# Expert tiles: one register load for three stagings, another order in the first steps, fewer products of zeros

## The chip, the cores and the metric

One core of a Trainium2 chip runs the whole program. Time is device microseconds from launch to end, median of three runs. TensorE is called PE, VectorE DVE, ScalarE ACT, GpSimd POOL, and SyncE SP.

## The reference

`x` is 4096 tokens of 256 features. The block is a macaron: half a mixture of experts, an attention with 16 heads, half the same mixture again.

```
def _L0_ffn_ref(x, gate_w, gate_b, w1, b1, w2, b2, w3, b3):
    logits = einsum('bsd,de->bse', x, gate_w) + gate_b
    probs = softmax(logits, axis=1)                 # over the 4096 tokens
    vals, idx = top_k(probs, 2)                     # 2 of 8 experts
    h = relu(einsum('bsd,edo->ebso', x, w1) + b1)
    h = relu(einsum('ebso,eop->ebsp', h, w2) + b2)
    y = relu(einsum('ebso,eop->ebsp', h, w3) + b3)
    v = einsum('ebso,bse->eo', y, w_tok)            # one row per expert
    return einsum('bse,eo->bso', ind, v)
x = x + 0.5 * ffn(layernorm(x))
x = x + attention(layernorm(x))
x = x + 0.5 * ffn(layernorm(x))
```

## The kernel before

The five engines run one program each, and semaphores order them. The first mixture (f = 0) lies at 35 to 301 us of the profiled execution, the attention at about 301 to 1950, the second mixture (f = 1) from there to the end.

A mixture has three parts. `route(f)` picks two experts per token and gives each of the 8192 (token, expert) pairs a slot, so that a tile of slots belongs to one expert. `tiles(f)` runs the three layers over 39 tiles: 32 wide ones of 256 slots and 7 narrow ones of 128, in the order of the table `ORDER`: one narrow tile first, then five or six wide ones and a narrow one, six times. Last come one row per expert and its addition to the tokens (`combine`).

Here is how one tile j passes through `tiles(f)`. Every engine walks steps 0 to 41 and touches several tiles in one step.

- POOL gathers the 128 rows of each half tile from DRAM (line 527). There are three slots, so the gather of tile j waits until tile j-3 was transposed and its weights were widened.
- PE transposes the rows (`transpose_tile`, line 1061, bank 0) and the widened weights (`transpose_weight`, line 1068, bank 1), and does the layers (`layer(f, j, l)`, line 1050, banks 2, 3 and 4 for l = 0, 1, 2). In fp32 each written product shows as two MATMULs, so a layer of a tile is four products and "x8" in the trace.
- ACT copies the transposed tile (line 806) and the weight row (line 810), does the first ReLU (line 817) and the last, summing one (line 801).
- DVE widens the weights of the tile (`widen_weight`, lines 1546, 1549, 1552), does the second ReLU (`relu_second`, line 1568), adds bias and weight after the third layer (`weigh`, line 1559), and copies one layer's weights of the tile's expert into one of two buffers (`stage(f, j, l)`). The expert's number is data: `value_load` (line 1534) brings it from SBUF into a register, and the copy (line 1535) takes its address from there.

Before step 0 PE waits through the last nine small DVE operations of `route`, with one product of zeros (128x512, line 1011) after each, and then does five more; the rows of tile 0 are gathered meanwhile. The gather can be issued once `row_no` is written, the second of these nine.

In step j, PE does layer 2 of tile j-3, the transposes of tile j, layer 1 of tile j-2, the weight transposes of tile j, layer 0 of tile j-1. DVE does `widen_weight(j)`, `weigh(j-3)`, `stage(j-1, 2)`, `relu_second(j-2)`, `stage(j, 1)`, `stage(j+1, 0)`. The last one waits for layer 0 of tile j-1 and for ACT's ReLU on it, since these read the buffer. Each engine keeps strictly to its written order.

Of the kernel before, what the change touches and what calls it, by code (L numbers as in the profile page):

```python
# [10 lines left out]
ACT = mybir.ActivationFunctionType  # L11
# [5 lines left out]
D = 256  # L17
NT = S // P
KD = D // P
H = 16  # L20
HD = D // H
E = 8
# [9 lines left out]
TILE = 256  # L32
# [6 lines left out]
N_TILES = WIDE + NARROW  # L39
# [5 lines left out]
W_RING = LAYERS + 1  # L45
# [67 lines left out]
FIRST_CHOSEN, FIRST_ROW = "chosen_bf", "row_scaled"  # L113
GATHER_FILL = 5


ORDER = [WIDE]
# [3 lines left out]
WIDTH = [P * len(subs) for subs in SUBS]  # L121

# [87 lines left out]
def subs_before(j):  # L210

    return sum(len(subs) for subs in SUBS[:max(j, 0)])
# [78 lines left out]
def macaron_block(nc, x_in, w_qkv_t, w_out_t, gate_w, gate_b, w1, w2, w3, bias_cols, out):  # L291
    with ExitStack() as ctx:
# [396 lines left out]
        def _(eng):  # L689
# [100 lines left out]

            def tiles(f):
                need.wait_ge(sig.inverse[f], TOP * NT)
                if f == 1:
                    need.wait_ge(sig.pv, PV_ALL)
                for n in range(N_TILES + LAYERS):
                    j = n - 3
                    if 0 <= j < N_TILES:
                        for m in range(KD):
                            need.wait_ge(sig.weighted[f], KD * j + m + 1)
                            tile, t = weighted[:, j % 2, m, 0:WIDTH[j]], ORDER[j]  # L800
                            eng.activation(tile, tile, ACT.Relu, accum_out=v_part[:, m, t:t + 1]).then_inc(sig.v_part[f], 1)  # L801
                    j = n
                    if j < N_TILES:
                        need.wait_ge(sig.xt[f], KD * subs_before(j + 1))
                        need.wait_ge(sig.layer[f][0], j - 1)
                        eng.activation(acts[:, 0, j % 2, :, 0:WIDTH[j]],
                                       bank[0][:, :].rearrange("p (k s) -> p k s", k=KD)[:, :, 0:WIDTH[j]], ACT.Copy).then_inc(sig.xt_copy[f], 1)
                        need.wait_ge(sig.w_tr[f], subs_before(j + 1))
                        need.wait_ge(sig.weighted[f], KD * (j - W_RING + 1))
                        eng.activation(w_row[:, j % W_RING, 0:WIDTH[j]], bank[1][:, 0:WIDTH[j]],  # L810
                                       ACT.Copy).then_inc(sig.w_row[f], 1)
                    j = n - 1
                    if 0 <= j < N_TILES:
                        need.wait_ge(sig.layer[f][0], j + 1)
                        need.wait_ge(sig.layer[f][1], j - 1)
                        for m in range(KD):
                            eng.activation(acts[:, 1, j % 2, m, 0:WIDTH[j]],  # L817
                                           bank[2][:, m * TILE:m * TILE + WIDTH[j]], ACT.Relu,
                                           bias=staged[:, j % 2, 0, KD * D + m:KD * D + m + 1],
                                           ).then_inc(sig.relu_a[f], 1)  # L820
# [95 lines left out]
        def _(eng):  # L916
# [154 lines left out]
            def tiles(f):  # L1071
                busy_beside(f, ROUTE[ROUTE.index(FIRST_ROW):])
                busy_beside(f, ROUTE[-1:] * GATHER_FILL)
                for j in range(N_TILES + LAYERS):
                    layer(f, j - 3, 2)
                    if j == 1:
                        layer(f, j - 1, 0)
                    if j < N_TILES:
                        transpose_tile(f, j)
                    layer(f, j - 2, 1)  # L1080
                    if j < N_TILES:
                        transpose_weight(f, j)
                    if j != 1:
                        layer(f, j - 1, 0)
                need.wait_ge(sig.v_part[f], KD * N_TILES)
                need.wait_ge(sig.routed[f], ROUTED["position"])
                for m in range(KD):
                    eng.transpose(bank[5][0:N_TILES, m * P:(m + 1) * P], v_part[:, m, :],
                                  ident[:, :]).then_inc(sig.v_tr[f], 1)
                need.wait_ge(sig.v_rows[f], 1)  # L1090
                need.wait_ge(sig.routed[f], ROUTED["tile_hot"])
                eng.matmul(bank[6][0:V_ROWS, 0:D], tile_hots[0:N_TILES, :], v_rows[0:N_TILES, :], start=True,
                           stop=True).then_inc(sig.v_mm[f], 1)
# [180 lines left out]
        def _(eng):  # L1274
# [244 lines left out]

            def stage(f, j, l):  # L1520
                if not 0 <= j < N_TILES:
                    return
                need.wait_ge(sig.routed[f], ROUTED["tile_exp_i"])
                need.wait_ge(sig.experts[f], 16 * (KD * LAYERS + 1))
# [6 lines left out]
                else:  # L1531
                    need.wait_ge(sig.weighted[f], KD * (j - 1))
                t = ORDER[j]
                expert = eng.value_load(tile_exp_i[0:1, t:t + 1], min_val=0, max_val=E - 1)
                eng.tensor_copy(staged[:, j % 2, l, :],  # L1535
                                experts[:, bass.ds(expert, 1), l, :].rearrange("p a w -> p (a w)"),
# [35 lines left out]
            def tiles(f):  # L1572
                stage(f, 0, 0)
                for j in range(N_TILES + LAYERS):
                    if j < N_TILES:
                        widen_weight(f, j)
# [6 lines left out]
                    stage(f, j + 1, 0)  # L1583
                need.wait_ge(sig.v_tr[f], KD)
# [134 lines left out]
```

## Time and profile before

| | us |
|---|---|
| median of three runs | 2230.15 (2228.54 to 2230.48) |
| the profiled execution's own time | 2234.71 |
| span of its trace | 2232.9 |
| PE busy | 2135.2 (96%) |
| DVE busy | 1846.4 (83%) |
| ACT busy | 1615.7 (72%) |
| POOL busy | 513.2 (23%) |

The page gives busy time per engine. Register loads are not counted in it; they show under DVEq, the sequencer of DVE, when their line is asked for. "Idle before <- X" at a row is the time that the engine stood still, and what ended it; "issue" means that the profile names no releaser. A row of several MATMULs shows the end of the last one, which lies a little behind the moment at which the next may start.

### The profile page before, as it was taken

The page shows a single profiled execution, that of the slowest core. Times are in us where ns is not written, and L with a number is a line of the kernel's source. Part 1 is how long each engine was busy: PE and PEld are TensorE (multiplying, and loading weights), DVE is VectorE, ACT ScalarE, POOL GpSimd, SP SyncE. Part 2 cuts the span into 40 slices and gives each one's busy share as a digit, 9 for nine tenths or more (in the row PEclk, how much of TensorE's full clock was granted, in tenths as well). Part 3 has the DMA queues.
Part 4 walks back from the last instruction along what each step waited for, and adds up shares of the span by engine and source line. Part 5 has one row for each costly group of instructions (what it writes and reads, how often), then busy time and mean ns, then how long its engine had stood idle before and what let it go on. Part 6 is the DMA issues. An engine that isn't in the chain of part 4 may idle for free.

```text
span 2232.9 us, 98125 instructions
## 1 busy us (share of the span) xinstructions
PE 2135.2 (96%) x42465; PEld 1845.8 (83%) x42469; DVE 1846.4 (83%) x3903; ACT 1615.7 (72%) x3556; POOL 513.2 (23%) x1295
## 2 busy tenths in 40 slices
PE   5999988999999999999999999999999999879997
PEld 3788855499999999999999899998999997658885
DVE  6655555899999999999999999999999994675555
ACT  5344445588888888888888888888888888334442
POOL 1333202422131221221212212222131210023330
PEclk8899989999999999999999999999999999979998
DMA  8211103310010110100101101010010101231112
GB/s 262 73 43 46 38 22 105 131 32 24 12 32 10 27 27 9 32 14 23 31 5 32 23 14 32 4 33 25 11 32 7 29 4 43 75 112 46 43 45 83
DMA packets 94855, 94.34 MB, mean 42 GB/s; under 512 B 41108, under 2 KB 83864, under 8 KB 94424
## 3 DMA queue, kind: packets, MB, share of 16 engines
q0 software_dynamic: 41376, 42.91, 7.5%
q1 hardware_dynamic: 52624, 45.15, 6.4%
q8 instruction: 334, 5.47, 1.0%
q14 instruction: 97, 0.79, 0.1%
q10 hardware_dynamic: 424, 0.01, 0.0%
HBM read 62.25 MB, written 25.43 MB: 39 GB/s over the span
## 4 chain that ended last, share of the span: by engine, by line
PE 88%; DVE 5%; issue 3%; ACT 1%; POOL 1%; DMA 1%; SPq 1%; DVEq 0%; ACTq 0%; POOLq 0%
PE bank L1154 44%; PE bank L1146 19%; PE bank L1050 17%; PE bank L1192 2%; PE bank L1061 1%; PE bank L1109 1%; PE bank L1257 1%; DVE stats L1287 1%; PE bank L1068 1%; PE bank L1200 1%; PE bank L1122 1%; SPq L646 0%; DVE rows L1309 0%; DVE x_res L1601 0%; DVE work L1476 0%
## 5 line engine op out<-in xcount | busy, mean ns | idle before, releaser
L1154 PE MATMUL bank<-work 96*32 96x512 bf16 (+4 forms) x17920 | 1413.8, 363 | 5.1 <-DVE work L1640 2.9
L869 ACT ACTIVATE feat<-bank 128x512 f32<-128x512 f32 (+3 forms) x2304 | 1251.4, 565 | 154.7 <-PE bank L1154 77.9
L1640 DVE TENSOR_REDUCE work<-bank 128x1 f32<-128x512 f32 (+3 forms) x2176 | 1300.0, 640 | 63.2 <-PE bank L1154 50.9
L1146 PE MATMUL bank<-feat,phase 128*17 128x128 f32 x16896 | 1136.8, 272 | 0.0
L1146 PEld LDWEIGHTS bank<-feat,phase 128*17 128x17 f32 x16896 | 828.7, 98 | 65.8 <-issue 1.6
L1154 PEld LDWEIGHTS bank<-work 96*32 96x32 bf16 (+1 forms) x17920 | 807.3, 96 | 72.7 <-DVE work L1640 11.5
L1050 PE MATMUL bank<-work 128*128 128x256 f32 (+1 forms) x1872 | 404.4, 363 | 14.2 <-issue 10.9
L1050 PEld LDWEIGHTS bank<-work 128*128 128x128 f32 x1872 | 319.1, 190 | 63.0 <-issue 19.3
L1535 DVE COPY work<-phase 128x514 f32 x234 | 103.8, 444 | 178.5 <-DVE work L1568 54.9
L585 POOL TENSOR_SCALAR_AFFINE_SELECT feat<-feat 128x128 f32<-128x128 f32 x512 | 146.3, 293 | 446.1 <-ACT feat L869 440.5
L527 POOL DMA_INDIRECT work<-token_table,row_no x142 | 135.5, 954 | 320.7 <-DVE work L1552 241.7
L801 ACT ACTIVATE work<-work 128x256 f32<-128x256 f32 (+1 forms) x156 | 60.6, 389 | 183.8 <-DVE work L1559 183.8
L592 POOL TENSOR_TENSOR rows<-work 128x64 f32<-128x64 f32 x128 | 37.3, 292 | 332.2 <-DVE work L1651 308.1
L817 ACT ACTIVATE work<-bank,work 128x256 f32<-128x256 f32 (+1 forms) x156 | 62.5, 452 | 69.3 <-PE bank L1050 69.3
L554 POOL DMA_DIRECT2D work<-qk_parts x180 | 106.7, 594 | 3.6 <-PE bank L1154 3.3
L576 POOL CAST work<-work 128x4 bf16<-128x4 f32 x128 | 23.8, 186 | 340.6 <-DVE work L1646 340.6
L1637 DVE TENSOR_REDUCE work<-bank 128x4 f32<-128x512 f32 x128 | 88.0, 688 | 0.5 <-PE bank L1200 0.5
L1192 PE MATMUL bank<-work 96*32 96x64 bf16 (+3 forms) x2048 | 84.3, 201 | 0.0
L1192 PEld LDWEIGHTS bank<-work 96*32 96x32 bf16 x2048 | 68.7, 95 | 8.8 <-issue 2.3
L1559 DVE SCALAR_TENSOR_TENSOR work<-bank,work 128x256 f32<-128x256 f32 (+1 forms) x156 | 64.1, 452 | 8.6 <-PE bank L1050 8.6
L1154 PE MATMUL bank<-ident,work 128*32 128x68 f32 x1024 | 70.5, 226 | 0.4 <-ACT work L885 0.4
L1568 DVE TENSOR_SCALAR work<-bank,work 128x256 f32<-128x256 f32 (+1 forms) x156 | 64.0, 452 | 0.0
(192 smaller groups left out, 1402.0 us busy)
## 6 DMA issues: line engine op xcount, KB each, us to landing
phase<-in_w SPq DMA_DIRECT2D x12, 1024.0 KB, 11.8
work<-qk_parts POOLq DMA_DIRECT2D x60, 192.0 KB, 3.7
token_table<-rows SPq DMA_DIRECT2D x8, 1056.0 KB, 8.7
qk_parts<-phase SPq DMA_DIRECT2D x20, 384.0 KB, 2.6
work<-qk_parts POOLq DMA_DIRECT2D x60, 128.0 KB, 4.2
qk_parts<-work SPq DMA_DIRECT2D x12, 384.0 KB, 2.6
x_res<-in_x SPq DMA_DIRECT2D x8, 512.0 KB, 8.7
work<-work SPq DMA_DIRECT2D x256, 1.0 KB
```

What stands on the lines that cost most here:

```text
L527: eng.indirect_dma_start(out=x_slot[:, j % NXG, u, :], out_offset=None, in_=table[f], in_offset=bass.IndirectOffsetOnAxis(ap=row_no[:, n:n ...
L554: eng.dma_start(stack[r * HD:(r + count) * HD, h % 2, c, tokens], src).then_inc(sig.stack[h % 2], 16)
L585: eng.affine_select(out=p_ring[:, n % P_RING, lo:lo + P], in_=p_ring[:, n % P_RING, lo:lo + P], compare_op=ALU.is_ge, fill=0.0, base=0, pa ...
L869: eng.activation(p_ring[:, n % P_RING, lo:QB], s_bank("probs", n)[:, lo:QB], ACT.Exp, scale=HD ** -0.5).then_inc(sig.s_done, 1)
L1050: mm = eng.matmul(bank[bk][:, m * TILE:m * TILE + WIDTH[j]], staged[:, b, l, k * D + m * P:k * D + (m + 1) * P], acts[:, l, b, k, 0:WIDTH[j]],
L1146: mm = eng.matmul(bank[ACC_BANK][GRID * g:GRID * g + VW, 0:P], v_aug[:, t, h, :], p_ring[:, n % P_RING, g * P:(g + 1) * P], start=(t == 0) ...
L1154: mm = eng.matmul(out[GRID * g:GRID * (g + 1), width], left[:, GRID * g:GRID * (g + 1)], right, start=start, stop=stop)
L1192: eng.matmul(tiles[GRID * g:GRID * (g + 1), i, 0:GRID * (g + 1)], stack[0:QK_ROWS, h % 2, 0, q0 + GRID * g:q0 + GRID * (g + 1)], stack[0:Q ...
L1535: eng.tensor_copy(staged[:, j % 2, l, :], experts[:, bass.ds(expert, 1), l, :].rearrange("p a w -> p (a w)"),).then_inc(sig.staged[f], 1)
L1559: eng.scalar_tensor_tensor(weighted[:, j % 2, m, 0:WIDTH[j]], bank[4][:, m * TILE:m * TILE + WIDTH[j]], staged[:, j % 2, 2, KD * D + m:KD ...
L1637: eng.tensor_reduce(maxima[:, h % 2, j, :, 0], scores[:, 0:QB].rearrange("p (i s) -> p i s", i=TPJ), AX_X, ALU.max).then_inc(sig.a_done, 1)
L1640: eng.tensor_reduce(maxima[:, h % 2, j, i, k + 1:k + 2], scores[:, 0:hi - lo], AX_X, ALU.max).then_inc(sig.a_done, 1)
```

## The change

Three edits, all in `tiles(f)` and so made twice in the program.

1. `stage` loads the expert's register only for l = 0 and keeps it for l = 1 and 2. The load now stands ahead of the waits of `stage(j+1, 0)`.
2. In steps 1 to 3 (`FIRST_STEPS`) PE does all layers first, and then the transposes of the incoming tile and its weights. ACT does its first ReLU ahead of the two copies. DVE does `widen_weight(j)` at the end of the step instead of at its start.
3. PE does 5 products of zeros instead of 14, and they wait for `row_no` alone.

```diff
-FIRST_CHOSEN, FIRST_ROW = "chosen_bf", "row_scaled"
+FIRST_CHOSEN = "chosen_bf"
...
+FIRST_STEPS = range(1, 4)
...
+                    relu_weighted(f, n - 3)
+                    if n in FIRST_STEPS:
+                        relu_first(f, n - 1)
+                    copy_tile(f, n)
+                    if n not in FIRST_STEPS:
+                        relu_first(f, n - 1)
...
-                busy_beside(f, ROUTE[ROUTE.index(FIRST_ROW):])
-                busy_beside(f, ROUTE[-1:] * GATHER_FILL)
+                busy_beside(f, ["row_no"] * GATHER_FILL)
                 for j in range(N_TILES + LAYERS):
                     layer(f, j - 3, 2)
-                    if j == 1:
+                    if j in FIRST_STEPS:
+                        layer(f, j - 2, 1)
                         layer(f, j - 1, 0)
+                        transpose_tile(f, j)
+                        transpose_weight(f, j)
+                        continue
                     if j < N_TILES:
                         transpose_tile(f, j)
                     layer(f, j - 2, 1)
                     if j < N_TILES:
                         transpose_weight(f, j)
-                    if j != 1:
-                        layer(f, j - 1, 0)
+                    layer(f, j - 1, 0)
...
+            expert_of = {}
+
             def stage(f, j, l):
                 if not 0 <= j < N_TILES:
                     return
                 need.wait_ge(sig.routed[f], ROUTED["tile_exp_i"])
+                t = ORDER[j]
+                if l == 0:
+                    expert_of[j] = eng.value_load(tile_exp_i[0:1, t:t + 1], min_val=0, max_val=E - 1)
                 need.wait_ge(sig.experts[f], 16 * (KD * LAYERS + 1))
...
-                t = ORDER[j]
-                expert = eng.value_load(tile_exp_i[0:1, t:t + 1], min_val=0, max_val=E - 1)
                 eng.tensor_copy(staged[:, j % 2, l, :],
-                                experts[:, bass.ds(expert, 1), l, :].rearrange("p a w -> p (a w)"),
+                                experts[:, bass.ds(expert_of[j], 1), l, :].rearrange("p a w -> p (a w)"),
...
-                    if j < N_TILES:
+                    if j < N_TILES and j not in FIRST_STEPS:
                         widen_weight(f, j)
...
                     stage(f, j, 1)
                     stage(f, j + 1, 0)
+                    if j in FIRST_STEPS:
+                        widen_weight(f, j)
```

On PE, the rows behind the weight transposes of step 0 and layer 0 of tile 0: steps 1 and 2 and the start of step 3, before. Bank 0 holds a tile's transposes, bank 1 its weights, banks 2, 3, 4 the layers 0, 1, 2.

```order
L1061 MATMUL bank0<-ident,work 128x128 x4
L1068 MATMUL bank1<-ident,work 128x128 x2
L1061 MATMUL bank0<-ident,work 128x128 x4
L1050 MATMUL bank3<-work 128x128 x4
L1068 MATMUL bank1<-ident,work 128x128 x2
L1050 MATMUL bank2<-work 128x256 x4
L1050 MATMUL bank4<-work 128x128 x4
L1061 MATMUL bank0<-ident,work 128x128 x4
L1050 MATMUL bank3<-work 128x256 x4
```

And with the change:

```order
L1075 MATMUL bank0<-ident,work 128x128 x4
L1082 MATMUL bank1<-ident,work 128x128 x2
L1064 MATMUL bank3<-work 128x128 x4
L1064 MATMUL bank2<-work 128x256 x4
L1075 MATMUL bank0<-ident,work 128x128 x4
L1082 MATMUL bank1<-ident,work 128x128 x2
L1064 MATMUL bank4<-work 128x128 x4
L1064 MATMUL bank3<-work 128x256 x4
L1064 MATMUL bank2<-work 128x256 x4
```

In step 2 the layers (bank 3, bank 2) moved ahead of both transposes of tile 2, and the weight transposes (bank 1) are now the last thing of the step, behind layer 0 of tile 1.

On DVE, from the last staging of step 1 to the second ReLU of step 2, before. TENSOR_LOAD and "ISA x2" are the load of the register, the single ISA works out the address, and the three rows from L1546 on widen the weights of tile 2:

```order
L1534 TENSOR_LOAD tile_exp_i
L1534 ISA x2
L1535 ISA
L1535 COPY work<-phase 128x514
L1546 TENSOR_TENSOR work<-work,feat 128x16
L1549 TENSOR_REDUCE work<-work 128x2
L1552 COPY work<-work 128x256
L1534 TENSOR_LOAD tile_exp_i
L1534 ISA x2
L1535 ISA
L1535 COPY work<-phase 128x514
L1568 TENSOR_SCALAR work<-bank3,work 128x128 x2
```

The same place with the change, from the last staging of step 1 on:

```order
L1544 TENSOR_LOAD tile_exp_i
L1544 ISA x2
L1554 ISA
L1554 COPY work<-phase 128x514
L1565 TENSOR_TENSOR work<-work,feat 128x16
L1568 TENSOR_REDUCE work<-work 128x2
L1571 COPY work<-work 128x256
L1554 ISA
L1554 COPY work<-phase 128x514
L1587 TENSOR_SCALAR work<-bank3,work 128x128 x2
L1554 ISA
L1554 COPY work<-phase 128x514
```

The three rows from L1565 on are now the widening of tile 1, which stood ahead of the stagings of step 1 and now closes that step; tile 2's comes at the end of step 2. Of three loads two are gone.

## Rows read from the trace of the kernel before

**Rows 1.** Page, part 1: busy us, share of span, instructions
```profile
PE 2135.2 (96%) x42465; PEld 1845.8 (83%) x42469; DVE 1846.4 (83%) x3903; ACT 1615.7 (72%) x3556; POOL 513.2 (23%) x1295
```

**Rows 2.** Busy by stretch (us and instructions), then granted clock, DMA share, GB/s
```profile
86.95:294.85 207.90, 202.10 (x1072) 173.33 (x1072) 121.20 (x360) 87.12 (x291) 57.17 (x60) 1.00 0.15 40
```

**Rows 3.** Waits of PE, 86.95 to 294.85: us in total, times, longest
```profile
PE bank L1050 <- issue: 5.4, 13, 0.6
```

**Rows 4.** Chain that ended last: start us, us, work in a row
```profile
78.50 0.89 PE bank L1050 x8
...
82.28 0.44 PE bank L1061 x4
82.72 1.73 PE bank L1050 x8
```

**Rows 5.** Timeline of PE, steady steps: start us, us, line, tile, count, idle before
```profile
106.69 1.89 PE L1050 MATMUL bank<-work 128*128 128x256 f32 x8
...
108.64 1.06 PE L1050 MATMUL bank<-work 128*128 128x128 f32 x8
110.08 1.97 PE L1050 MATMUL bank<-work 128*128 128x256 f32 x8 [0.38 <-issue]
...
294.88 1.13 PE L1050 MATMUL bank<-work 128*128 128x128 f32 x8 [0.75 <-DVE work L1568]
```

**Rows 6.** Timeline of DVE, same stretch
```profile
108.76 0.43 DVE L1535 COPY work<-phase 128x514 f32 x1 [0.77 <-DVE work L1559]
109.11 0.87 DVE L1568 TENSOR_SCALAR work<-bank,work 128x256 f32<-128x256 f32 x2
```

**Rows 7.** Line 1534, then 1535, on DVE and its sequencer (DVEq): ns min/median/max
```profile
L1534 DVEq TENSOR_LOAD <-tile_exp_i x234: 297/304/554, 68.9 to 2203.8; - x117
L1534 DVEq FUSED_REGOPS  x234: 190/190/216, 69.5 to 2204.1; - x117
L1535 DVEq FUSED_REGOPS  x234: 65/69/75, 70.2 to 2204.4; - x117
```

**Rows 8.** Timeline of all engines, start of the first tile stage
```profile
69.79 3.59 PE L1011 MATMUL bank<-zeros_bf 128*128 128x512 bf16 x13 [0.22 <-issue]
...
71.26 0.17 DVE L1546 TENSOR_TENSOR work<-work,feat 128x8 f32<-128x8 f32 x1 [0.33 <-DMA work<-token_table,row_no]
...
71.66 0.32 DVE L1552 COPY work<-work 128x128 f32<-128x128 f32 x1
...
74.22 1.13 PE L1050 MATMUL bank<-work 128*128 128x128 f32 x8 [0.52 <-ACT work L806]
...
76.58 0.63 ACT L817 ACTIVATE work<-bank,work 128x128 f32<-128x128 f32 x2
...
78.05 0.51 DVE L1535 COPY work<-phase 128x514 f32 x1 [1.81 <-ACT work L817]
...
78.06 0.44 PE L1061 MATMUL bank<-ident,work 128*128 128x128 f32 x2 [1.15 <-DMA work<-token_table,row_no]
...
81.43 0.84 ACT L817 ACTIVATE work<-bank,work 128x256 f32<-128x256 f32 x2 [1.35 <-PE bank L1050]
...
86.98 1.97 PE L1050 MATMUL bank<-work 128*128 128x256 f32 x8 [0.58 <-issue]
```

**Rows 9.** The same, second tile stage
```profile
1985.46 0.17 DVE L1546 TENSOR_TENSOR work<-work,feat 128x8 f32<-128x8 f32 x1 [1.45 <-DMA work<-token_table,row_no]
...
1988.61 1.13 PE L1050 MATMUL bank<-work 128*128 128x128 f32 x8 [0.52 <-ACT work L806]
...
2001.29 1.97 PE L1050 MATMUL bank<-work 128*128 128x256 f32 x8 [0.58 <-issue]
```

**Rows 10.** Busy by stretch and granted clock, at and after changes of the clock
```profile
75.00:80.00 5.00, 3.38 (x27) 2.83 (x26) 2.28 (x8) 2.29 (x6) 3.72 (x5) 1.00 0.42 111
1905.00:1910.00 5.00, 2.42 (x15) 1.63 (x13) 4.62 (x21) 2.27 (x5) 0.00 (x0) 1.00 1.13 311
1910.00:1915.00 5.00, 5.00 (x16) 4.10 (x17) 1.13 (x2) 0.00 (x0) 0.00 (x0) 0.66 0.22 7
```

More of the change, by code:

```diff
@@ L789, in route, with relu_weighted, copy_tile, relu_first @@
                                    ACT.Copy).then_inc(sig.chosen_copy[f], 1)
+            def relu_weighted(f, j):
+                if not 0 <= j < N_TILES:
+                    return
+                for m in range(KD):
+                    need.wait_ge(sig.weighted[f], KD * j + m + 1)
+                    tile, t = weighted[:, j % 2, m, 0:WIDTH[j]], ORDER[j]
+                    eng.activation(tile, tile, ACT.Relu, accum_out=v_part[:, m, t:t + 1]).then_inc(sig.v_part[f], 1)
+            def copy_tile(f, j):
+                if j >= N_TILES:
+                    return
+                need.wait_ge(sig.xt[f], KD * subs_before(j + 1))
+                need.wait_ge(sig.layer[f][0], j - 1)
+                eng.activation(acts[:, 0, j % 2, :, 0:WIDTH[j]],
+                               bank[0][:, :].rearrange("p (k s) -> p k s", k=KD)[:, :, 0:WIDTH[j]],
+                               ACT.Copy).then_inc(sig.xt_copy[f], 1)
+                need.wait_ge(sig.w_tr[f], subs_before(j + 1))
+                need.wait_ge(sig.weighted[f], KD * (j - W_RING + 1))
+                eng.activation(w_row[:, j % W_RING, 0:WIDTH[j]], bank[1][:, 0:WIDTH[j]],
+                               ACT.Copy).then_inc(sig.w_row[f], 1)
+            def relu_first(f, j):
+                if not 0 <= j < N_TILES:
+                    return
+                need.wait_ge(sig.layer[f][0], j + 1)
+                need.wait_ge(sig.layer[f][1], j - 1)
+                for m in range(KD):
+                    eng.activation(acts[:, 1, j % 2, m, 0:WIDTH[j]], bank[2][:, m * TILE:m * TILE + WIDTH[j]], ACT.Relu,
+                                   bias=staged[:, j % 2, 0, KD * D + m:KD * D + m + 1]).then_inc(sig.relu_a[f], 1)
             def tiles(f):
@@ L795, in tiles @@
                 for n in range(N_TILES + LAYERS):
[L796 to L802, printed above, removed]
-                    if j < N_TILES:
[L804 to L820, printed above, removed]
+                    relu_weighted(f, n - 3)
[4 more added lines that the diff above has]
+                        relu_first(f, n - 1)
             def part1(n, projected):
@@ L1574, in tiles @@
                 for j in range(N_TILES + LAYERS):
-                    if j < N_TILES:
+                    if j < N_TILES and j not in FIRST_STEPS:
                         widen_weight(f, j)
```

## The prediction

> **What bounds the kernel now.** I began with the page. PE is busy for 96% of the span, DVE for 83% [rows 1]. PE is the engine that sets the end, so time can only be saved where PE stands still. The attention is untouched by the diff. That leaves the two tile stages.
>
> Next I split a tile stage. From layer 2 of tile 1 (the first work of step 4, 86.98) to layer 2 of the last tile (294.88) PE counts as busy for 202.10 of 207.90 us [rows 2], and its waits name 5.4 us in 13 pieces, none over 0.6 [rows 3]. Busy rows include the tails of pipelined products, so I count the work itself. The chain shows a wide layer of 8 products at 1.73 us when work follows at once, a narrow one at 0.89, four transposes at 0.44, so 0.11 each [rows 4]. A wide tile is 3 x 1.73 + 6 x 0.11 = 5.85 us, a narrow one 3 x 0.89 + 3 x 0.11 = 3.00. A stage is 32 x 5.85 + 7 x 3.00 = 208.2 us. Before 86.98 lie three narrow layers, three wide ones and 21 transposes, 10.2 us; behind 294.88 lies 0.9. In the 207.9 us between are thus 197.1 us of work, and PE loses 10.8 us there.
>
> The third view says to whom. Layer 1 of a tile starts at 106.69 and is through at 108.58; a narrow layer 0 runs from 108.64; the wide layer 2 that is next starts only at 110.08 [rows 5]. It needs the second ReLU of DVE, which runs 109.11 to 109.98, 0.53 later than its input allowed. Ahead of it stands a staging copy that began at 108.76 after 0.77 us of idle DVE [rows 6]. In that idle time the sequencer loads the expert's register: 0.30 us for the load, 0.19 for the operations on it, then 0.07 for the address [rows 7]. So here DVE, which the page calls idle, is late with register loads, and PE waits for it beside each narrow tile, where PE's own step is short.
>
> The fourth view is the start of a stage. Tile 0's rows are there at 71.26, but PE still does products of zeros (13 in 3.59 us from 69.79), and layer 0 of tile 0 starts at 74.22. Then PE waits for a gather until 78.06. Step 4 starts at 86.98 [rows 8], in the second stage at 2001.29, after a layer 0 at 1988.61 [rows 9].
>
> **Part 1, the register.** 234 loads become 78. Each one removed takes 0.30 + 0.19 = 0.49 us out of DVE's order; the 0.07 for the address stays. Per step DVE gets 2 x 0.49 = 1.0 us back, and the load that remains stands ahead of the waits of its staging, so it runs while DVE waits anyway: after ACT's first ReLU ends at 77.21 the copy now starts at 78.05, 0.84 later [rows 8]; with the load out of the way I take 0.84 - 0.49 = 0.35. At the place of rows 5 and 6 two loads lie between the previous step's end and the ReLU, 1.0 us, where 0.53 is enough. The ReLU then starts at 108.61 and ends at 109.48, PE starts 0.10 later at 109.58, and its order alone would have had it there at 108.64 + 0.89 = 109.53. What is late next is PE itself. What stays of the 10.8 us is about 0.15 at each narrow tile, 0.9 in six, and the end, where too little work is left to cover ReLU and layer in turn: 0.75 us idle plus 0.16 of tail before 294.88 [rows 5], and some 0.35 at the layer before. That is 2.2, a saving of 8.6. I take 8.2, as ACT's work now bunches too. Bounds: at least the 5.4 us of named waits less the 0.9 at the end, 4.5; at most all of 10.8. Two stages: -16.4 us, between -9 and -21.6.
>
> **Part 2, the zeros.** 9 products of zeros fewer, and no wait for the operations behind `row_no`. The fifth one ends about 71.45 (one stands ahead of 69.79, and four follow at 0.43 us each, the pace of 512 columns at 1.2 GHz). PE then does tile 0's transposes as soon as the rows are there: two transposes, the copy by ACT, and layer 0 of tile 0 starts near 72.4 instead of 74.22, 1.8 us earlier. In the second stage the rows are there at 1985.46 [rows 9], and by the same 1.14 us layer 0 starts at 1986.6 instead of 1988.61, 2.0 earlier.
>
> **Part 3, the order of steps 1 to 3.** It removes a wait: layers at hand fill the 1.15 us in which PE waited for the gather. It adds another. The weight transposes now close a PE step; they wait for the widening, which now stands behind `stage(j+1, 0)` on DVE; and this copy waits for layer 0 of tile j-1 and for ACT's ReLU on it, both of the same step. Queued behind the waiting transposes on PE are all layers of the next step. The chain of one such step, from rows 4, 5, 6 and 8: layer 0 is through (1.89 from its start if wide), 0.05, ReLU 0.84 wide or 0.63 narrow, 0.35 to the copy, 0.35 until the next may follow it, widening 0.72 (71.26 to 71.98), 0.10 to PE, transposes 0.22. Walked through for the first stage:
> - Step 1: layer 0 of tile 0 at 72.40, through at 73.53; ReLU until 74.21; copy 74.56; widening 74.91 to 75.63; weight transposes 75.73 to 75.95.
> - Step 2: layer 1 of tile 0 (0.89) and layer 0 of tile 1, through at 78.73; ReLU until 79.62; copy 79.97; widening 80.32 to 81.04; 81.14 to 81.36. PE stands still from 79.0 to 81.1.
> - Step 3: layers 0.89 + 1.73 and the last one through at 85.87; ReLU 86.76; copy 87.11; widening 87.46 to 88.18; step 4 at 88.50.
>
> That is 16.1 us from layer 0 of tile 0 to step 4, where it was 12.8 (74.22 to 86.98). So the earlier start of part 2 is used up: step 4 comes at 88.5 instead of 86.98, 1.5 later. In the second stage 1986.6 + 16.1 = 2002.7 against 2001.29, 1.4 later. The two stages: +2.9 us. The nearest bound below is that the chain hides altogether and the 1.8 and 2.0 us stay: -3.8. Above, a narrower slot for the gathers (tile 6's waits for the widening of tile 3, now 88.2) costs nothing, as two gathers and their landing would have until step 6.
>
> **The clock.** Steps 2 and 3 now hold pauses of about 2.1 us. Near 1905 to 1910 PE was busy for 2.42 of 5 us, and in the 5 us after that the granted clock reads 0.66; in 75 to 80 it was busy 3.38 of 5 us with pauses, and it stayed at 1.00 [rows 10]. The new steps, with 2.6 to 4.4 us of work beside 2.1 of pause, lie between the two. A fall like the first costs at most 5 x (1 - 0.66) = 1.7 us, the part of those 5 us that the clock withheld. I take one fall in the two stages, +1.7; none gives 0, two give 3.4, and a late rise after the shorter run of zeros up to 2 more.
>
> On this the Trainium skill (TensorE: Matmul & The Clock Gate, HAM oscillation) says that a kernel whose matrix engine waits between bursts can find the gate closed after each wait, so that every burst begins at half clock. By that rule both stages pay, which is the second rival's time; the trace of before has one place that goes with it and one that does not.
>
> **Sum.** -16.4 + 2.9 + 1.7 = -11.8 us. The profiled execution took 2234.71, so the same with the change is 2222.9; its runs had a median of 2230.15, 4.6 less, which gives 2218.4. I say 2218.5.
>
> **Rivals.**
> - The moved steps pay. For it: PE's waits at the start did have a gather and two ACT copies at their end. Against it: the chain above, which has no slack in it. Then 2230.15 - 16.4 - 3.8 = 2210.
> - The clock costs more: a fall in each stage and a late rise after the zeros, +3.4 + 2 instead of +1.7. For it: the pauses recur in three steps in a row. Against: 75 to 80. Then 2222.
> - Slower than before: the clock stays at 1.2 GHz from layer 0 of tile 0 until the steady steps in both stages, because the longer run of zeros was what raised it. PE's work there, 10.2 - 0.3 = 9.9 us, doubles each time: -16.4 + 2.9 + 19.8 = +6.3, so 2236. It decides once the rise comes later than some 7 us of PE's work into each stage (2 x 7 = 14 against the 13.5 that parts 1 to 3 give). Against it: at 1.2 GHz the work itself fills the pauses, and the clock did rise within the zeros: 13 of them took 3.59 us, where 1.2 GHz throughout makes 5.5 and 2.4 GHz makes 2.8.
> - The change doesn't do what it says: the copies still start 0.8 us after what they wait for, since something else than the load fills that time. Then parts 2 and 3 and the clock are left: 2230.15 + 4.6 = 2235. Against it: 0.30 + 0.19 + 0.07 accounts for 0.56 of 0.77, at 234 loads alike.
>
> **How the numbers follow.** Forecast 0.60, moved steps pay 0.12, dearer clock 0.18, clock low throughout 0.06, loads not the cause 0.04. The forecast's own spread is 2214 to 2222. Half of the first rival and all of the second within reach give 2212 to 2226; the two slow cases stay out. 0.2% of this kernel is 4.5 us, about what a measurement can tell from no change. The first three cases are faster by more, save their upper edge: faster 0.88, within 0.2% 0.04, slower 0.08.
>
> **What will show it.** Right: TENSOR_LOAD x78; the idle time of DVE before the copies at 0.25 to 0.35 instead of 0.77 where they wait for DVE's own results; PE's named waits between step 4 and the last tile under 2 us instead of 5.4, and that stretch near 200 us instead of 207.9 in each stage; the weight transposes of tiles 1, 2 and 3 waiting for the widening copy, about 1.4, 2.1 and 2.1 us; step 4 later than 86.98 although layer 0 of tile 0 is earlier. Wrong: step 4 earlier than 85 (the first rival), granted clock under 1.00 between 71 and 95 over more than 4 us (the second or third), or copies that still follow at 0.77 (the last).

## The result, and the profile after

| | before | changed |
|---|---|---|
| median of the runs, us | 2230.32 (2228.54 to 2230.85, 4 runs) | 2215.78 (2212.90 to 2220.74, 4 runs) |
| ratio, 95% interval | 1 | 0.9928, [0.9913, 0.9943] |
| profiled execution: time, span, us | 2234.71, 2232.9 | 2220.74, 2218.7 |
| `row_no` to step 4, first / second stage | 19.36 / 19.76 | 20.58 / 20.76 |
| step 4 to layer 2 of the last tile | 207.90 / 208.14 | 198.85 / 198.85 |

The kernel is 14.5 us faster; 11.8 were forecast (2218.5). The forecast lies 2.7 us above the measured median, which is inside its range. In the two profiled executions the span shrinks by 14.2 us: the steady steps of the two stages give 9.05 + 9.29 = 18.3, their starts take back 1.22 + 1.00 = 2.2, and 1.9 is lost where the diff changes nothing (0.5 ahead of the first stage, 1.0 between the stages, 0.4 at the end).

The same rows as ahead of the prediction, now of the changed kernel. The page, part 1, answers to [rows 1], and shows almost nothing of this:

```profile
PE 2123.2 (96%) x42447; PEld 1848.4 (83%) x42451; DVE 1849.8 (83%) x3903; ACT 1619.5 (73%) x3556; POOL 515.5 (23%) x1295
```

The steady stretch of the first stage, against [rows 2] (us, then busy time of PE, PEld, DVE, ACT, POOL, then clock, DMA share, GB/s):

```profile
88.71:287.56 198.85, 197.97 (x1075) 175.29 (x1073) 122.39 (x356) 89.00 (x291) 58.94 (x61) 1.00 0.16 42
```

and PE's waits in it, against [rows 3] (us in total, times, longest). The 13 waits of 5.4 us are gone; the 1.7 is the tail of step 3, the 0.7 the last layer of all:

```profile
PE bank L1082 <- DVE work L1571: 1.7, 1, 1.7
PE bank L1064 <- DVE work L1587: 0.7, 1, 0.7
```

DVE at the place that answers to [rows 6]: weighing, copy, second ReLU, two copies. The copy after the weighing (109.37) and the one after the ReLU (111.02) follow with no idle time that the view prints (the ReLU ends at 110.88), where it was 0.77 us. DVE now waits for PE and ACT, not they for it:

```profile
108.36 0.87 DVE L1578 SCALAR_TENSOR_TENSOR work<-bank,work 128x256 f32<-128x256 f32 x2
109.37 0.43 DVE L1554 COPY work<-phase 128x514 f32 x1
110.00 0.88 DVE L1587 TENSOR_SCALAR work<-bank,work 128x256 f32<-128x256 f32 x2 [0.20 <-PE bank L1064]
111.02 0.63 DVE L1554 COPY work<-phase 128x514 f32 x1
```

The register loads, against [rows 7] (ns min/median/max; DVEq is DVE's sequencer):

```profile
L1544 DVEq TENSOR_LOAD <-tile_exp_i x78: 299/304/554, 69.4 to 2180.4; - x78
L1544 DVEq FUSED_REGOPS  x78: 190/190/216, 70.0 to 2180.7; - x78
```

PE at the start of the first stage, against [rows 8], and step 4 of the second, against [rows 9]:

```profile
73.12 1.13 PE L1064 MATMUL bank<-work 128*128 128x128 f32 x8
...
76.22 0.44 PE L1082 MATMUL bank<-ident,work 128*128 128x128 f32 x2 [1.43 <-DVE work L1571]
76.50 2.79 PE L1064 MATMUL bank<-work 128*128 128x128 f32 x16
...
81.47 0.44 PE L1082 MATMUL bank<-ident,work 128*128 128x128 f32 x2 [1.75 <-DVE work L1571]
81.74 4.51 PE L1064 MATMUL bank<-work 128*128 128x128 f32 x24
...
88.44 0.44 PE L1082 MATMUL bank<-ident,work 128*128 128x128 f32 x2 [1.75 <-DVE work L1571]
88.71 1.89 PE L1064 MATMUL bank<-work 128*128 128x256 f32 x8
...
1995.97 1.25 PE L1064 MATMUL bank<-work 128*128 128x256 f32 x5
```

The wait for the gather at 78.06 has gone; in its place stand three waits of the weight transposes for the widening copy, 4.9 us in all. Their reason is in DVE's rows: the staging copy of tile 3's layer 0 waits for ACT's ReLU until 80.37, the widening (three operations) can only follow it, and PE's transposes at 81.47 stand behind that.

```profile
80.37 0.43 DVE L1554 COPY work<-phase 128x514 f32 x1 [1.60 <-ACT work L821]
80.71 0.17 DVE L1565 TENSOR_TENSOR work<-work,feat 128x16 f32<-128x16 f32 x1
80.91 0.17 DVE L1568 TENSOR_REDUCE work<-work 128x2 f32<-128x16 f32 x1
81.12 0.29 DVE L1571 COPY work<-work 128x256 f32<-128x256 f32 x1
```

The clock through these pauses, against [rows 10]: 1.00, in the slices with pauses too.

```profile
80.00:85.00 5.00, 3.53 (x21) 3.27 (x22) 2.45 (x9) 1.72 (x7) 2.10 (x3) 1.00 0.28 71
85.00:90.00 5.00, 3.25 (x18) 2.68 (x17) 2.40 (x10) 1.71 (x4) 0.87 (x1) 1.00 0.09 27
```

### The profile page after: what moved, and what is told of

It is laid out like the page before. It is cut to its first block, busy times and chain, and to the rows that moved or that the text cites. A ratio compares the mean times of both kernels' runs of the same rounds, so it can differ in the third digit from the quotient of the medians.

```text
span 2218.7 us, 97623 instructions
## 1 busy us (share of the span) xinstructions
PE 2123.2 (96%) x42447; PEld 1848.4 (83%) x42451; DVE 1849.8 (83%) x3903; ACT 1619.5 (73%) x3556; POOL 515.5 (23%) x1295
## 4 chain that ended last, share of the span: by engine, by line
PE 89%; DVE 5%; issue 2%; ACT 2%; POOL 1%; DMA 1%; SPq 1%; DVEq 0%; ACTq 0%; POOLq 0%
PE bank L1170 44%; PE bank L1162 19%; PE bank L1064 17%; PE bank L1208 2%; PE bank L1075 1%; PE bank L1125 1%; PE bank L1273 1%; DVE stats L1303 1%; PE bank L1082 1%; PE bank L1216 1%; PE bank L1138 1%; SPq L649 0%; DVE rows L1325 0%; DVE x_res L1622 0%; DVE work L1492 0%
## 5 line engine op out<-in xcount | busy, mean ns | idle before, releaser
L1064 PE MATMUL bank<-work 128*128 128x256 f32 (+1 forms) x1872 | 395.3, 361 | 2.0 <-DVE work L1587 1.5
L1208 PE MATMUL bank<-work 96*32 96x32 bf16 (+3 forms) x2048 | 84.2, 201 | 0.1
```

Of the source, the lines that this page charges most:

```text
L1064: mm = eng.matmul(bank[bk][:, m * TILE:m * TILE + WIDTH[j]], staged[:, b, l, k * D + m * P:k * D + (m + 1) * P], acts[:, l, b, k, 0:WIDTH[j]],
L1208: eng.matmul(tiles[GRID * g:GRID * (g + 1), i, 0:GRID * (g + 1)], stack[0:QK_ROWS, h % 2, 0, q0 + GRID * g:q0 + GRID * (g + 1)], stack[0:Q ...
```

## The experiments

Eleven kernels, each timed in five rounds against the kernel before on its own chip. "Start" is `row_no` to step 4, "steady" is step 4 to the last tile's layer 2, both for the first / second stage of the profiled execution, read from the timelines; step 4 is layer 2 of tile 1, and `row_no` is the start of the DVE operation that writes it. The recorded expectations of loads_zeros and after_14_zeros call the zeros edit 2 and the order edit 3, the other way round than the list of the change.

| kernel | loads, place | order | zeros | median us | ratio, 95% interval | start | steady |
|---|---|---|---|---|---|---|---|
| before | 3, behind | old | 14 | 2230.3 | 1 | 19.4 / 19.8 | 207.9 / 208.1 |
| changed | 1, ahead | new | 5 | 2215.8 | 0.9928 [0.9913, 0.9943] | 20.6 / 20.8 | 198.9 / 198.9 |
| loads_only | 1, ahead | old | 14 | 2211.9 | 0.9911 [0.9898, 0.9924] | 18.2 / 18.1 | 198.8 / 198.8 |
| three_ahead | 3, ahead | old | 14 | 2209.5 | 0.9910 [0.9896, 0.9924] | 18.9 / 18.1 | 198.8 / 198.8 |
| one_behind | 1, behind | old | 14 | 2216.1 | 0.9928 [0.9915, 0.9942] | 18.5 / 18.5 | 199.5 / 200.3 |
| six_behind | 6, behind | old | 14 | 2348.4 | 1.0520 [1.0506, 1.0535] | 23.3 / 23.7 | 262.3 / 263.1 |
| order_zeros | 3, ahead | new | 5 | 2220.9 | 0.9958 [0.9946, 0.9970] | 21.8 / 23.7 | 198.9 / 198.9 |
| order_zeros_behind | 3, behind | new | 5 | 2247.8 | 1.0069 [1.0056, 1.0083] | 26.5 / 26.6 | 209.5 / 209.7 |
| loads_zeros | 1, ahead | old | 5 | 2209.1 | 0.9893 [0.9879, 0.9908] | 16.8 / 16.9 | 198.8 / 198.8 |
| after_14_zeros | 1, ahead | new | 14 | 2222.4 | 0.9936 [0.9921, 0.9950] | 23.1 / 22.6 | 198.8 / 198.9 |
| widen_before_copy | 1, ahead | new, widening up one place | 5 | 2213.5 | 0.9896 [0.9881, 0.9912] | 18.9 / 18.9 | 198.9 / 198.9 |
| early_no_zeros | 1, ahead | new, widening first | 0 | 2216.0 | 0.9906 [0.9891, 0.9921] | 19.3 / 18.6 | 198.9 / 198.8 |
| widen_early | 1, ahead | new, widening first | 5 | 2204.2 | 0.9879 [0.9865, 0.9894] | 15.7 / 15.6 | 198.9 / 198.9 |

For widen_before_copy, early_no_zeros and after_14_zeros the kernel before took 2237.8 us on their chip, 2231 on the others; so their ratios, not their medians, are compared with the rest. "Ahead" and "behind" are against the semaphore waits of the staging that uses the register.

### Part 1 alone: loads_only

```diff
 # kernel before, stage(f, j, l)
+ if l == 0: expert_of[j] = eng.value_load(...)   # ahead of the waits
  need.wait_ge(...)                               # experts, layer, relu / weighted
- expert = eng.value_load(...)
- eng.tensor_copy(staged[...], experts[:, bass.ds(expert, 1), ...])
+ eng.tensor_copy(staged[...], experts[:, bass.ds(expert_of[j], 1), ...])
```

> Edit 1 alone on the kernel before: one register load a tile, old order of steps 1 to 3, 14 products of zeros. Theory A (PE's lost time in the steady steps is DVE's register loads, and the reordered start costs about 1 us a stage): the stretch from step 4 to the last tile's layer 2 falls from 207.9 to about 198.9 us in each stage, step 4 comes 0.3 to 1.0 us earlier than before, and the time is 2209 to 2213, 2 to 5 us below the changed kernel. Rival B (a good part of the gain comes from the new start, the zeros or the order, and the loads are not all of it): the steady stretch stays over 203 us and the time is 2221 or more.

Measured 2211.92 with a steady stretch of 198.8: theory A. This edit alone saves 19 us, more than the whole change. Step 4 comes 1.2 and 1.7 us earlier than before, a little more than the 0.3 to 1.0 expected.

### Parts 2 and 3 with three loads: order_zeros

```diff
 # changed kernel
- if l == 0:
+ if True:
      expert_of[j] = eng.value_load(...)
```

> Edits 2 and 3 alone: the changed kernel with three register loads a tile as before. Theory A: the steady stretch stays near 207.9 us, step 4 comes 2 to 3.5 us later than before in each stage (the chain through the widening copy now holds register loads as well), and the time is 2233 to 2237. Rival B: the stretch shortens without the loads being gone, or step 4 is earlier, and the time is 2222 to 2229.

Neither theory; of theory A only the later step 4 came, 2.5 and 4.0 us behind the kernel before. 2220.85 is 10 us faster than before, although 234 loads run, and the steady stretch is 198.85 as in the changed kernel. The edit had left the loads where the changed kernel has them: ahead of the waits. So in the steady steps the number of loads doesn't matter there, and what the prediction had priced, 0.49 us for each load taken out, could not be the reason. That called for the next four kernels.

In the starts the number does matter. Step 4 comes 1.2 and 3.0 us later than in the changed kernel, and the intervals of the two ratios, 0.9958 and 0.9928, don't touch. In steps 0 and 1 DVE's staging copies follow one another with nothing to wait for. With a load ahead of each they come every 0.76 us (74.74, 75.50). Without it three of them, from 73.26, take 1.11 us in the changed kernel, one every 0.34. The widening stands behind them, and PE's first wait for it is 2.68 us where it was 1.43, and 3.05 where it was 1.59 in the second stage. Behind the 3.05 the clock fell as well (0.76 in 1978 to 1983).

```profile
74.74 0.43 DVE L1554 COPY work<-phase 128x514 f32 x1 [0.33 <-issue]
75.50 0.43 DVE L1554 COPY work<-phase 128x514 f32 x1 [0.33 <-issue]
...
77.65 0.44 PE L1082 MATMUL bank<-ident,work 128*128 128x128 f32 x2 [2.68 <-DVE work L1571]
...
1979.56 0.44 PE L1082 MATMUL bank<-ident,work 128*128 128x128 f32 x2 [3.05 <-DVE work L1571]
```

### Place or number: three_ahead and one_behind

```diff
 # three_ahead: kernel before, stage(f, j, l)
+ expert = eng.value_load(...)
  need.wait_ge(...)
- expert = eng.value_load(...)
  eng.tensor_copy(...)
```

> The kernel before with one thing changed: each of the 234 stagings still loads its register, but ahead of the staging's waits instead of behind them. Theory P (place: a load behind the waits cannot run under DVE's own weighing or ReLU, ahead of them it does): the steady stretch falls to 198.9 us as with 78 loads, copies follow 0.15 us after DVE's own results, and the time is 2209 to 2214. Theory N (number: each load takes 0.49 us out of DVE's order wherever it stands, as the prediction had it): the stretch stays over 205 us and the time is 2226 or more.

2209.46, steady 198.84, in the kernel before with one line moved and all 234 loads kept. The copy follows DVE's own weighing by 0.15 us where it was 0.77. So it is at 142 of the 148 copies for which the trace names a result of DVE's own as what ended the wait:

```profile
105.79 0.87 DVE L1559 SCALAR_TENSOR_TENSOR work<-bank,work 128x256 f32<-128x256 f32 x2
106.81 0.43 DVE L1535 COPY work<-phase 128x514 f32 x1 [0.15 <-DVE work L1559]
```

The loads are all there, and as long as before:

```profile
L1525 DVEq TENSOR_LOAD <-tile_exp_i x234: 297/304/556, 68.7 to 2177.7; - x117
```

They now run while DVE still weighs or does its ReLU. Behind the waits they can't: the staging waits for the result of DVE's own operation just ahead of it, so the sequencer stands until that has ended, and only then loads. A load behind the waits thus costs 0.62 us at each copy (0.77 - 0.15), not 0.49. For the steady steps theory P is right, and theory N, the prediction's own account, is wrong.

```diff
 # one_behind: kernel before, stage(f, j, l)
  need.wait_ge(...)
+ if l == 0: expert_of[j] = eng.value_load(...)   # still behind the waits
- expert = eng.value_load(...)
  eng.tensor_copy(...)
```

> The kernel before with one register load a tile (78 instead of 234), left where it was, behind the waits of the first staging of the tile. Theory P: this load stands behind a wait for ACT's first ReLU, and its copy is not what PE waits for next, so little is lost either way; steady stretch 198.9 to 200 us, time 2211 to 2216. Theory N: the same, 198.9 to 200. If instead the stretch is over 203 us, the place of this one load, not of the two others, was what cost, and both are wrong.

Steady 199.5 and 200.3, 2216.14 us: a single load behind the waits costs about 1 us a stage, as expected, the second value slightly over the range. The copy of layer 0 starts 0.83 us after the end of ACT's ReLU (104.16 to 104.99), with the load ahead of the waits 0.21 us after it (103.99 to 104.20 in loads_only). That is 0.62 us again, and PE hardly needs the copy then:

```profile
104.99 0.43 DVE L1538 COPY work<-phase 128x514 f32 x1 [1.84 <-ACT work L817]
```

The gain can thus be had in two ways, by number or by place; the changed kernel does both, and either is enough for nearly all of it: one_behind keeps 0.7 and 1.4 us more in the steady stretches than loads_only.

### What a load behind the waits costs: six_behind

```diff
 # kernel before, stage(f, j, l)
- expert = eng.value_load(...)
+ for _ in range(2):
+     expert = eng.value_load(...)
```

> The kernel before with every register load made twice, behind the waits (468 loads; the second repeats the first). It sizes a load in that place. Theory P and N: at the narrow tiles, where PE's step is short, each staging ahead of the second ReLU is late by another 0.49 us, 1.0 us at each of 7 places, and in the wide steps the slack of DVE against PE's 5.85 us is used up in part, so the steady stretch is 215 to 222 us in each stage and the time 2245 to 2262. If it stays under 2238, loads behind waits are cheap and the gain comes from something else in the edit.

2348.36, over 85 us beyond the expected range; 109 of the 117 us that it costs lie in the steady stretches. The wide steps (here from 177.27 to 184.57) now take 7.30 us instead of PE's 5.85:

```profile
177.27 1.96 PE L1050 MATMUL bank<-work 128*128 128x256 f32 x8 [1.04 <-DVE work L1536]
...
184.57 0.67 PE L1050 MATMUL bank<-work 128*128 128x256 f32 x2 [1.23 <-DVE work L1536]
```

DVE's idle time before its three copies of a step says what a load costs. In six_behind:

```profile
104.18 0.43 DVE L1536 COPY work<-phase 128x514 f32 x1 [1.39 <-issue]
...
106.79 0.43 DVE L1536 COPY work<-phase 128x514 f32 x1 [1.40 <-issue]
108.25 0.43 DVE L1536 COPY work<-phase 128x514 f32 x1 [1.03 <-issue]
```

In the kernel before, behind the copy at 108.76 with its 0.77 [rows 6]:

```profile
110.74 0.43 DVE L1535 COPY work<-phase 128x514 f32 x1 [0.77 <-DVE work L1568]
111.58 0.43 DVE L1535 COPY work<-phase 128x514 f32 x1 [0.40 <-issue]
```

Each further load adds 0.62 or 0.63 us, as in three_ahead and one_behind, 1.88 us a step. DVE's whole wide step, from one copy of layer 0 to the next, is 5.42 us in the kernel before (106.16 to 111.58, where DVE waits for no other engine) and 7.29 in six_behind (100.96 to 108.25). So the slack that both theories gave DVE was there, 5.85 - 5.42 = 0.43 us a wide step. Their mistake was the size: with 1.88 us more, DVE sets the pace of every wide step and not only of those beside a narrow tile. Its busy share tells nothing of it: in this stretch of six_behind, where DVE sets the pace, it counts as busy for 13.46 of 30 us.

```profile
150.00:180.00 30.00, 23.55 (x128) 19.46 (x127) 13.46 (x41) 9.14 (x32) 7.80 (x8) 1.00 0.13 37
```

### Part 1 wholly undone: order_zeros_behind

```diff
 # changed kernel, stage(f, j, l)
- if l == 0: expert_of[j] = eng.value_load(...)
  need.wait_ge(...)
+ expert_of[j] = eng.value_load(...)
  eng.tensor_copy(...)
```

> The changed kernel with the register edit wholly undone: three loads a tile, each behind its staging's waits as in the kernel before; new order and five products of zeros stay. Both theories: the steady stretch is back at 207.9 us, step 4 comes 2 to 4 us later than in the kernel before in each stage, and the time is 2233 to 2240, slower than before. If it is 2229 or less, the new order does not cost what the difference between the changed kernel and the one with the old order says.

Slower than before, as expected, but by 17 us instead of 2 to 9. The steady stretch is 209.5, and step 4 comes 7 us later than in the kernel before. The loads now stand in the chain through the widening, whose waits grow to 2.75, 2.38 and 2.38 us, and behind each of these the clock falls, in both stages: the two layers at 77.15 take 4.46 us, where the same 16 products take 2.79 in the changed kernel (76.50).

```profile
76.88 0.44 PE L1082 MATMUL bank<-ident,work 128*128 128x128 f32 x2 [2.75 <-DVE work L1570]
77.15 4.46 PE L1064 MATMUL bank<-work 128*128 128x128 f32 x16
...
84.43 0.54 PE L1082 MATMUL bank<-ident,work 128*128 128x128 f32 x2 [2.38 <-DVE work L1570]
84.77 6.11 PE L1064 MATMUL bank<-work 128*128 128x128 f32 x24
```

```profile
75.00:80.00 5.00, 3.12 (x15) 2.77 (x16) 2.49 (x9) 0.38 (x1) 3.80 (x4) 0.78 0.41 110
80.00:85.00 5.00, 2.62 (x13) 2.05 (x12) 1.30 (x5) 1.32 (x3) 0.00 (x0) 0.84 0.12 29
85.00:90.00 5.00, 5.00 (x21) 4.50 (x21) 1.85 (x5) 1.08 (x5) 1.89 (x2) 0.70 0.19 56
```

This is the prediction's second rival, at work in another kernel. The parts don't add up: the new order with its fewer zeros costs 17 us beside loads behind the waits, and about 4 beside one load ahead of them (2215.8 against 2211.9).

### The order taken out: loads_zeros, and the zeros: after_14_zeros

```diff
 # loads_zeros: kernel before with part 1 and
- busy_beside(f, ROUTE[ROUTE.index(FIRST_ROW):])
- busy_beside(f, ROUTE[-1:] * GATHER_FILL)
+ busy_beside(f, ["row_no"] * GATHER_FILL)
 # after_14_zeros: the changed kernel with these lines the other way round
```

> Edits 1 and 2 (one register load a tile, five products of zeros), with the old order of steps 1 to 3 on all engines. Theory A: the order is the part that costs; without it the earlier layer 0 of tile 0 is kept in part, step 4 comes 1 to 3 us earlier than in the changed kernel in each stage, steady stretch 198.9 as there, time 2208 to 2213. Rival B (the new order pays for itself, filling PE's wait for the gather): step 4 no earlier than in the changed kernel and the time 2216 or more. Rival C (fewer zeros cost clock): granted clock under 1.00 for over 4 us in the first steps, time 2214 to 2222.

2209.12, step 4 at 16.8 us behind `row_no` instead of 20.6: theory A, with more than the 1 to 3 us expected (3.8 and 3.9). Against loads_only the five zeros give 2.8 us in the medians, which the intervals don't tell apart, and 1.4 + 1.2 us in the starts. Against the changed kernel the old order gives 6.7 us in the medians and 3.8 + 3.9 us in the starts. The new order, as made, is the part that costs.

> The changed kernel with the 14 products of zeros of before, that is edits 1 and 3 without edit 2. If the prediction's part 2 holds, layer 0 of tile 0 comes 1.6 to 2.0 us later than in the changed kernel in each stage, nothing behind it has slack, step 4 is later by the same, and the time is 2218 to 2221. If the waits behind it absorb it (gather or widening chain), it is 2214 to 2217.

Layer 0 of tile 0 comes 7.47 and 6.95 us behind `row_no` instead of 4.99 and 5.11, and step 4 is later by as much, 2.5 and 1.8. In the starts this is 4.3 us, as part 2 of the prediction had it and more. The ratio 0.9936 against 0.9928 doesn't tell the two kernels apart; the intervals overlap.

### The widening moved back: widen_early and widen_before_copy

```diff
 # widen_early: changed kernel, DVE's tiles(f)
- if j < N_TILES and j not in FIRST_STEPS:
+ if j < N_TILES:
      widen_weight(f, j)
  ...
  stage(f, j + 1, 0)
- if j in FIRST_STEPS:
-     widen_weight(f, j)
```

> The changed kernel with one thing put back: in steps 1 to 3 the widening of the gate weights stands at the start of DVE's step, as in all other steps, while PE and ACT keep the new order. Theory A: PE's waits of 1.4 to 1.8 us for the widening copy in front of the weight transposes of tiles 1, 2 and 3 go, step 4 comes 3 to 4.5 us earlier in each stage (about 84.5 instead of 88.7 in the first), and the time is 2206 to 2210, the lowest of all. Rival B (the waits only move: DVE now stands behind the gathers in its order, and PE waits for the gather or for the second ReLU instead): step 4 at most 1.5 us earlier, time 2213 to 2216.

2204.15, the fastest of all and a little below the range of theory A, with the new order on PE and ACT kept. The three waits are gone, but for 0.53 us in step 1 of the second stage, and step 4 comes 4.9 and 5.2 us earlier than in the changed kernel (3 to 4.5 were expected):

```profile
74.44 0.44 PE L1082 MATMUL bank<-ident,work 128*128 128x128 f32 x2
74.74 2.86 PE L1064 MATMUL bank<-work 128*128 128x128 f32 x16
...
77.87 0.38 PE L1082 MATMUL bank<-ident,work 128*128 128x128 f32 x2
78.09 4.51 PE L1064 MATMUL bank<-work 128*128 128x128 f32 x24
...
83.09 1.89 PE L1064 MATMUL bank<-work 128*128 128x256 f32 x8
```

So the new order on PE and ACT is no loss: its start is 1.1 and 1.3 us shorter than with the old order (loads_zeros). The loss lay in DVE's half of it.

```diff
 # widen_before_copy: changed kernel, DVE's tiles(f)
  stage(f, j, 1)
+ if j in FIRST_STEPS:
+     widen_weight(f, j)
  stage(f, j + 1, 0)
- if j in FIRST_STEPS:
-     widen_weight(f, j)
```

> The changed kernel with the widening in steps 1 to 3 moved up by one place only on DVE: ahead of the staging copy of the next tile's layer 0 (which waits for ACT's first ReLU), behind the other copies and the second ReLU. If the copy's wait for ACT is the whole of PE's 1.4 to 1.8 us waits, as the prediction's chain has it, this is as fast as the widening at the start of the step: 2203 to 2207, step 4 15.6 to 16.2 us behind row_no. If what stands further ahead (weighing, second ReLU, two copies) is part of it, step 4 comes 17 to 20 us behind row_no and the time is 2208 to 2214.

Step 4 comes 18.9 us behind `row_no`: the second case by the place of step 4. The time doesn't decide between the cases: the ratio of 0.9896 makes 2207 where the kernel before takes 2230. 1.7 and 1.9 of the 4.9 and 5.2 us are won by passing the copy that waits for ACT; the waits in steps 1 and 3 are down to 0.6 us or gone. The one in step 2 stays, 1.8 us, for the widening still stands behind the second ReLU, and that began late:

```profile
78.24 0.61 DVE L1587 TENSOR_SCALAR work<-bank,work 128x128 f32<-128x128 f32 x2 [2.38 <-remote]
```

```profile
81.14 0.84 ACT L821 ACTIVATE work<-bank,work 128x256 f32<-128x256 f32 x2 [5.49 <-remote]
```

By PE's rows the layers that these two wait for ran in a row from 75.07 to 77.86. For what ended the two waits the trace says only "remote", which names no instruction, and it is the same in the second stage. Why they came so late is open, and with it how much the copy alone is worth.

### No zeros at all: early_no_zeros

```diff
 # widen_early with
- GATHER_FILL = 5
+ GATHER_FILL = 0
```

> The changed kernel with the widening at the start of all steps, and with none of the five products of zeros. PE has then nothing to do between the chosen rows and tile 0's rows (about 2 us). Clock theory (the zeros keep or bring up the granted clock for the first layers, as the prediction's slow rival had it): granted clock under 1.00 over more than 4 us of the first steps in one or both stages, step 4 two to ten us later, time 2207 to 2224. Rival (they are idle filling by now, since tile 0's rows end the wait): clock as with them, time 2203 to 2206.

The clock theory. Step 4 comes 3.6 and 3.0 us later than in widen_early. The first layers run at 1.2 GHz: the granted clock is 0.50 and 0.61 in the first two rows below, and 8 narrow products take 2.05 us in both stages, where widen_early took 1.40 and 1.13. Up to the weight transposes of step 2 this makes 1.9 and 2.0 us. The rest lies behind them: PE waits once more for DVE's second ReLU (1.42 us at 82.59 in the first stage), which again begins late with "remote" as what released it, as in widen_before_copy. So not all of the 3.6 and 3.0 us is shown to be the clock.

```profile
70.00:75.00 5.00, 2.93 (x14) 2.14 (x13) 2.23 (x8) 1.63 (x4) 3.79 (x5) 0.50 0.38 98
75.00:80.00 5.00, 5.00 (x24) 4.78 (x24) 2.50 (x9) 1.50 (x4) 3.78 (x5) 0.61 0.40 111
```

```profile
73.50 2.05 PE L1064 MATMUL bank<-work 128*128 128x128 f32 x8 [0.21 <-issue]
```

The five zeros fill a wait that is there without them, but they bring the clock up.

## Why the prediction was right, and where it was not

**Part 1, the register: the place and the sign right, the reason wrong in the steady steps.** Forecast -8.2 us a stage, measured -9.05 and -9.29, -18.3 instead of -16.4. That PE waits for DVE beside the narrow tiles, and that DVE waits there for its own register load, both hold. But the step that said "each one removed takes 0.30 + 0.19 = 0.49 us out of DVE's order" failed. What frees DVE is that no load is left behind a wait for DVE's own last result; three loads ahead of the waits give the same 198.84 us as one. Nor is 0.49 us the size: behind the waits a load costs 0.62 us, and the copies now follow DVE's own results by 0.14 us, not by the 0.25 to 0.35 expected. Only where copies follow one another without a wait, in the starts with the new order, does the number of loads count (order_zeros). The prediction had the right mechanism in hand, but used it for the remaining load only ("stands ahead of the waits of its staging, so it runs while DVE waits anyway"). The size was off by about 1 us a stage: 1.75 us of the 10.8 stay (198.85 - 197.1) where 2.2 was taken, and the 0.4 us set aside for ACT's bunching was not needed; the second stage had lost 0.2 us more to begin with.

**Part 2, the zeros: right.** Layer 0 of tile 0 comes 1.61 and 1.97 us earlier against `row_no` (forecast 1.8 and 2.0).

**Part 3, the order: right, a little too dear.** From layer 0 of tile 0 to step 4 it took 15.6 us in both stages, forecast 16.1. The waits were 1.43, 1.75 and 1.75 instead of 1.4, 2.1 and 2.1: the copy follows ACT's ReLU by 0.21 us (80.16 to 80.37), not by 0.35. So the two starts lost 2.2 us against a forecast of 2.9. That the wait stood behind the widening is shown by widen_early. That it was all due to the copy waiting for ACT is not: with the copy alone out of the way, 1.8 us of waiting stay in step 2, for the reason left open above.

**The clock: wrong by 1.7.** No fall came in either start. The Trainium skill (TensorE: Matmul & The Clock Gate, HAM oscillation) has a kernel whose matrix engine waits for data between bursts and finds its gate closed after each wait; the waits there are longer than these. Behind waits of 1.4 to 1.8 us the changed kernel's trace shows no such fall (1.00 from 75 to 95). Behind waits of 2.38 to 3.02 the trace of order_zeros_behind does, each time (0.78, 0.84 and 0.70 from 75 to 90 in the first stage). The length of one wait doesn't settle it alone: in order_zeros the clock stayed at 1.00 behind a wait of 2.68 us in the first stage and fell behind one of 3.05 in the second.

**What no term held.** 1.9 us came from stretches that the diff leaves alone. Between the last tile of the first stage and `row_no` of the second the profiled executions of kernels with the same code there took 1681.0 us (order_zeros) to 1687.7 (changed), before 1686.7. That is the scatter of one execution, and no effect of the edits is to be read in it.

**Rivals.** "The moved steps pay" (2210) fell as a forecast of this kernel, but on PE's side it was right: they do pay once DVE's widening stays where it was, and then the time is 2204. "The clock costs more" and "the clock stays low" fell; both mechanisms exist, in order_zeros_behind and, for part of the start, in early_no_zeros. "The loads are not the cause" fell with loads_only.

## What to carry to other kernels

Put a register load ahead of the semaphore waits of the instruction that uses it: behind them it can't overlap the engine's own work, and 0.62 us a load is then added to its order, unseen in the busy share. Where the instructions follow one another without a wait, load once: even ahead of the waits a load cost some 0.4 us there. When steps are reordered on one engine, leave the feeders of the moved step where they were on the others: here the new order on PE and ACT was worth 1 us a stage, and the move on DVE cost 5. Before calling an engine idle, double its suspected cost once: the trace of that one run gave the price of a load and how little slack DVE had, 0.43 us in a step of 5.85.

## What the runs showed of the hardware

- A register load on DVE is 304 ns plus 190 ns of register operations (medians of 234, the longest load 556 ns), whether DVE is busy or not. Behind the waits it costs 0.62 us: DVE's copies follow its own results by 0.77 us instead of 0.15 (three_ahead) and ACT's by 0.83 instead of 0.21 (one_behind against loads_only), and three more loads make a wide step of DVE 7.29 us instead of 5.42 (six_behind). Ahead of the waits it costs nothing that can be measured as long as DVE has something to wait for (three_ahead against loads_only: 0.9910 and 0.9911); between copies that wait for nothing it costs 0.42 us (0.76 against 0.34, order_zeros against the changed kernel).
- None of it counts as busy: DVE's busy time was 1846.4 us before and 1849.8 after, with 156 loads fewer.
- In the starts PE kept the full clock through waits of 1.43 to 1.75 us in three steps in a row, and in order_zeros through one of 2.68. It lost it behind one of 3.05 there, and behind all six waits of 2.38 to 3.02 in order_zeros_behind.
- After a stretch without products ahead of the first layers (1.86 us in early_no_zeros) it began them at 1.2 GHz, the level it had had before, and reached 2.4 GHz in the layers of step 2. With five products of zeros in that stretch it reached 2.4 GHz within them or, at the latest, in the first layer (widen_early, first stage, where that layer took 1.40 us).
